# Keep x whole where it was first loaded, and take five of the eight row blocks of the residual sum from there instead of loading them a second time

## The reference, cut to what matters

```python
def L0(V, adj):      # N = 8192, D = 128
    return (adj == 1) @ (V @ w1) + (adj == 2) @ (V @ w2) + (adj == 3) @ (V @ w3) + bias
def L1(X, adj):
    h = X @ W.T + b
    e = leaky(h @ we1 + be1 + (h @ we2 + be2).T)      # slope 0.01
    return softmax(where(adj > 0, e, -9e15), axis=1) @ h
x = layernorm(x + L0(x, adj))
x = layernorm(x + L1(x, adj))
```

## Time and profile before

| what | value |
|---|---|
| median of 3 runs | 1555.93 us (1555.51 to 1557.21) |
| the profiled execution's own time | 1557.76 us |
| its span | 1556.1 us |
| PE busy | 1418.2 us, 91% |
| DVE busy | 1106.7 us, 71% |
| ACT busy | 981.2 us, 63% |
| mean granted TensorE clock | 0.979 |
| loads of 512 KB `x_rows<-x` | 8, median 7.2 us from issue to landing |

### The profile page before, as it was taken

How to read it: one execution, slowest core, us unless ns; L and a number is a source line. 1 busy time by engine, 2 the same in 40 slices (tenths; PEclk the granted TensorE clock), 3 DMA queues, 4 the chain that set the end, 5 groups by cost and what they waited for, 6 DMA issues and landing times. The chain is left out here.

```text
span 1556.1 us, 19556 instructions
## 1 busy us (share of the span) xinstructions
PE 1418.2 (91%) x6934; PEld 669.7 (43%) x6934; DVE 1106.7 (71%) x2561; ACT 981.2 (63%) x1584; POOL 102.2 (7%) x137
## 2 busy tenths in 40 slices
PE   0887798979999999999999997999999999999996
PEld 0434343444444444444444443444444444444443
DVE  2667777877977967967967946577667676666663
ACT  1334527446457457457457558678888788788873
POOL 2111111100110110100101000000000000000000
PEclk9989899999999999999999998999999999999998
DMA  9999999994979779886889421000110000100100
GB/s 125 145 126 116 130 107 140 115 108 76 83 100 115 83 74 102 114 83 75 113 85 102 82 95 55 8 1 28 48 34 28 28 28 27 55 27 28 35 1 15
DMA packets 88980, 114.32 MB, mean 73 GB/s; under 512 B 5104, under 2 KB 71216, under 8 KB 88880
## 3 DMA queue, kind: packets, MB, share of 16 engines
q0 software_dynamic: 67584, 67.12, 47.1%
q1 hardware_dynamic: 21296, 45.92, 8.6%
HBM read 298.06 MB, written 16.29 MB: 202 GB/s over the span
## 5 line engine op out<-in xcount | busy, mean ns | idle before, releaser
L1234 PE MATMUL ps<-pos_masks,tables 128*128 128x512 fp8e4 x2048 | 613.6, 381 | 39.6 <-DVE pos_masks L616 39.6
L1023 ACT ACTIVATE neg_masks<-e_row,cols 128x512 int8<-128x512 f32 x816 | 509.8, 709 | 109.0 <-PE ps L1234 58.4
L1234 PE MATMUL ps<-neg_masks,tables 128*128 128x512 fp8e4 x1632 | 489.7, 382 | 0.0
L1187 PE MATMUL ps<-edge_masks,tables 128*128 128x512 fp8e4 (+1 forms) x2048 | 463.9, 385 | 0.0
L1234 PEld LDWEIGHTS ps<-pos_masks,tables 128*128 128x128 f16 x2048 | 199.6, 98 | 285.8 <-issue 57.0
L1187 PEld LDWEIGHTS ps<-edge_masks,tables 128*128 128x128 f16 x2048 | 201.6, 99 | 233.2 <-issue 13.3
L1234 PEld LDWEIGHTS ps<-neg_masks,tables 128*128 128x128 f16 x1632 | 160.6, 98 | 195.8 <-issue 5.5
L614 DVE TENSOR_TENSOR neg_masks<-pos_masks,neg_masks 128x2048 uint16<-128x2048 uint16 x102 | 125.0, 1225 | 92.6 <-ACT neg_masks L1023 89.9
L598 DVE TENSOR_SCALAR pos_masks<-edges 128x512 uint16<-128x512 uint16 x512 | 114.4, 286 | 89.4 <-PE ps L1234 89.4
L1002 ACT ACTIVATE packed_bf<-packed 128x1024 bf16<-128x1024 uint8 x64 | 72.3, 1130 | 149.4 <-DVE packed L588 149.4
L598 DVE TENSOR_SCALAR edge_masks<-edges 128x512 uint16<-128x512 uint16 x512 | 124.2, 308 | 54.4 <-PE ps L1187 53.4
(11 more groups left out here) (134 smaller groups left out, 850.5 us busy)
## 6 DMA issues: line engine op xcount, KB each, us to landing
adj_in<-adj POOLq DMA_DIRECT2D x84, 512.0 KB, 13.7
tables<-adj POOLq DMA_DIRECT2D x28, 512.0 KB, 32.3
e_row<-e_scratch SPq DMA_DIRECT2D x34, 256.0 KB, 3.9
edges<-adj POOLq DMA_DIRECT2D x16, 512.0 KB, 12.5
part_scratch<-a_c_rows SPq DMA_DIRECT2D x18, 256.0 KB, 4.1
part_in<-part_scratch SPq DMA_DIRECT2D x18, 256.0 KB, 3.1
edges<-x SPq DMA_DIRECT2D x8, 512.0 KB, 6.6
x_rows<-x SPq DMA_DIRECT2D x8, 512.0 KB, 7.2
```

Source lines behind the costliest of these rows:

```text
L1023: ins = e.activation(gate_bufs[GATE[m]][:, n:n + GR].bitcast(I8), e1row[:, q % 2, :], ACT.Sign, bias=t2[:, JC * c + j:JC * c + j + 1])
L1187: ins = e.matmul(ps[:, h, :], v_hl[:, i, JC * c + j, :], U0[:, n:n + GR].bitcast(kind), start=c == 0 and j == 0 and i == 0, stop=c == NCH ...
L1234: ins = e.matmul(z_bank(q, k), tab[:, c, 2 * k + i, j, :], mask[:, n:n + GR].bitcast(F8A), start=first and j == 0 and i == 0, stop=final a ...
```

## The change

`split_rest` no longer writes over `x_in`. It writes the rest into `yT8`, which is the buffer `yT` (`y_turned` in the trace, free until slot 9) seen as 8 x 128, and `split_low` reads it there. There is one such buffer for all eight pieces, so `split_rest(v)` also waits until `split_low(v - 1)` is done. `x_in` stays whole until `edges_of` writes edge blocks 4 to 7 over it. `x_and_bias(S)` for S below `KEPT = 5` reads `x_in`, and the five loads `xg_load(0)` to `xg_load(4)` are gone; those for S = 5, 6 and 7 stay. `edges_of(k)` from k = 32 on waits for four, from k = 48 on for five `x_and_bias`. As `xg` is now written by DVE where a transfer wrote it, `x_and_bias(S)` waits for `e_sums(S - 1)`.

```diff
--- before.py
+++ after.py
@@ -105,6 +105,8 @@
 ASK = [max(-1 if p is None else p for p in LAST[:k + 1]) for k in range(K)]
 GUEST = {n: max(k for k in range(K) if HOME[k] == n) for n in (2, 3, 4)}
 AFTER = 9
+
+KEPT = 5
 
 STAGED = (4, 5, 6)
 
@@ -383,7 +385,6 @@
                 if v > 1:
                     e.wait_ge(s_adj[HOME[v - 2]], 32 * FILL[v - 2])
                 x_piece(v)
-            xg_load(0)
 
             def tail(S):
                 e.wait_ge(s_x1, S + 1)
@@ -399,7 +400,8 @@
                         e.dma_start(tab_dram[S - 4, n], (yT, xg)[n][:, :, :].rearrange("p a b -> p (a b)"))\
                             .then_inc(s_tabst, 16)
                     e.wait_ge(s_tabst, 16 * (2 * (S - 3)))
-                xg_load(S + 1)
+                if S + 1 >= KEPT:
+                    xg_load(S + 1)
 
             def row_of(q):
                 g = SEGS[q][0]
@@ -566,7 +568,8 @@
             def split_rest(v):
                 sl = slice(v * JC, (v + 1) * JC)
                 e.wait_ge(s_vh, v + 1)
-                e.tensor_tensor(x_in[:, sl, :], x_in[:, sl, :], v_hl[:, 0, sl, :], ALU.subtract).then_inc(s_vr, 1)
+                ge(e, s_vl, v)
+                e.tensor_tensor(yT8, x_in[:, sl, :], v_hl[:, 0, sl, :], ALU.subtract).then_inc(s_vr, 1)
 
             def check_and_pack(k):
                 e.wait_ge(s_adj[HOME[k]], 32 * FILL[k])
@@ -617,9 +620,15 @@
 
 
             def x_and_bias(S):
-                e.wait_ge(s_xg, 16 * (S + 1))
+                if S < KEPT:
+                    e.wait_ge(s_x, 16 * (S + 1))
+                    ge(e, s_er, S)
+                    rows = x_in[:, S * JC:(S + 1) * JC, :]
+                else:
+                    e.wait_ge(s_xg, 16 * (S - KEPT + 1))
+                    rows = xg[:, :, :]
                 e.wait_ge(s_w, W_ALL)
-                e.tensor_tensor(xg[:, :, :], xg[:, :, :], biases[:, 0:D].unsqueeze(1).broadcast_to([P, RB, D]),
+                e.tensor_tensor(xg[:, :, :], rows, biases[:, 0:D].unsqueeze(1).broadcast_to([P, RB, D]),
                                 ALU.add).then_inc(s_xb, 1)
 
             def v_of(S, h):
@@ -994,7 +1003,7 @@
             def split_low(v):
                 sl = slice(v * JC, (v + 1) * JC)
                 e.wait_ge(s_vr, v + 1)
-                e.activation(v_hl[:, 1, sl, :], x_in[:, sl, :], ACT.Copy, scale=LOW).then_inc(s_vl, 1)
+                e.activation(v_hl[:, 1, sl, :], yT8, ACT.Copy, scale=LOW).then_inc(s_vl, 1)
 
             def convert(k):
                 e.wait_ge(s_pk, k + 1)
@@ -1006,6 +1015,7 @@
                 e.wait_ge(s_turn, k + 1)
                 if k >= 4 * NCH:
                     e.wait_ge(s_vl, NCH)
+                    e.wait_ge(s_xb, KEPT if k >= 6 * NCH else 4)
                 if k >= (NS - 1) * NCH:
                     e.wait_ge(s_pk, GUEST[4] + 1)
                 e.activation(bits_of(k // NCH, k % NCH), psT, ACT.Copy).then_inc(s_evac, 1)
```

## The result

| | before | after |
|---|---|---|
| median of 20 runs each, us | 1555.95 | 1553.67 |
| lowest and highest, us | 1552.58, 1558.86 | 1550.6, 1556.67 |
| span of the profiled execution, us | 1556.1 | 1554.1 |
| mean granted clock of PE | 0.979 | 0.979 |

The ratio of after to before is 0.9985, with a 95% interval from 0.9978 to 0.9992. The changed kernel is 2.3 us faster (1.2 to 3.4), where 2.0 had been forecast. The interval does not reach no change; the forecast had held anything under 0.2% (3.1 us) for too small to tell.

A forecast was written before the change was run, and what follows sets the result against it. Up to 142 us the DMA engines set the slot time, behind that the chain through DVE, ACT and PE. -1.3 - 0.7 = -2.0 us takes 1555.93 to 1553.9 us; range 1552.0 to 1556.4 us.

The forecast's parts named there:

- The removed load of block 0: At chunk 6, where DVE waits for each chunk: it comes 1.32 us sooner and the shift stays, -1.3 us.
- The first rival: In slot 6 the chunk loads need something besides DMA engines, so freed time stays empty: 1555.2 to 1555.9 us, chance 0.14.
- A sooner landing of the first `e_row`: Around 159 us, without `xg_load(1)` behind it, the load ACT waits for lands sooner: -0.7 us.
- I take half of the upper end: At the first `e_row`: upper end 1.5 us (4.5 against 3.0 us) for 512 KB behind; 256 KB follows now, so 0.7 us.
- The other four loads: Loads of blocks 1 to 4, where DVE never waits for a chunk: worth 0, but for the first of them.
- it is hidden by the work of slots that take longer than 9.90 us: Up to 778 us: the 5.3 us of transfer of blocks 1 to 4 counts as 0.
- Added waits, other buffer: In `split_rest`, `x_and_bias` and `edges_of`: new waits already met, subtraction still 1223 ns, cost 0; at worst 1.3 us for asking.
- The slower rival: `edges_of(32)` hangs on `x_and_bias(3)`, deciding if DVE comes over 6.5 us later against ACT: 1557.4 us if 10 late, chance 0.04.
- the larger gain: At slot 13, ACT's 2.98 us wait gone and PE perhaps keeping its clock: 4.3 or 7.2 us, some 1551.6 us, chance 0.17.
- The rival of unlucky meetings: Saved time returns as another wait, e.g. `e_row` meeting a chunk load, up to 2.9 us: around 1555.9 us, chance 0.07.
- The growth behind 190 us: Sign against the forecast: a kernel difference growing after 190 us, forecast as -2.0 us there and at the end.

The follow-up runs named there:

- kept1: Against the kernel before, only the load of block 0 is removed, with the added waits of `edges_of` left: 1555.48 us, ratio 0.9993.
- load0_back: The changed kernel with the load of block 0 put back, its data unused: 1554.73 us, ratio 0.9985 to the kernel before.
- load0_again: The changed kernel with the load of block 0 put back, timed a second time: 1553.72 us, ratio 0.998 to the kernel before.
- after_again: The changed kernel, unaltered, measured once more: 1552.62 us, ratio 0.9976 to the kernel before on the same chip.
- kept0_timed: The kernel before with all eight loads, only the subtraction's target and the waits of `split_low` and `edges_of` changed: 1556.92 us, ratio 1.0.

## Why the prediction was right in its sum and wrong in two terms

- **The removed load of block 0, -1.3 us: right.** Every trace without this load has a slot 5 of 11.23 or 11.24 us, and every one with it 12.56 to 12.58. Four loads more cost four times the price. The first rival, that the DMA engines lose what they win, fell here. Alone the load is worth 1.1 us by the ratio of `kept1` (from 2.5 us gained to 0.3 lost), which agrees but would not have shown it.
- **A sooner landing of the first `e_row`, -0.7 us: wrong.** The step that failed is "I take half of the upper end", above all the upper end itself, read from a pair taken on emptier DMA engines: their share was 0.74 in the 4.5 us from 368.5 us and 0.25 in the 3.0 us from 723.1 us, against 1.11 in the 6.0 us from 159 us. On full ones the load takes 5.9 to 6.3 us with anything or nothing behind it. The rule of the Trainium skill, DMA: Bandwidth & Descriptors, section Queues, rings and completion order, which I had weighed lower, agrees with the runs there. On emptier engines the landing did get shorter without the load of `x` behind (4.5 us at 368.5 us before, 3.3 us after; 4.0 to 4.9 us in six traces with the load behind and 3.0 to 3.3 us in five without), nearly as the upper end had it, but no engine waited for it.
- **The other four loads, 0: wrong.** The step that failed is "it is hidden by the work of slots that take longer than 9.90 us". The medians of kernels without them, against those with them, give: `load0_back` -2.5, `load0_again` -3.2, `after_again` against `kept1` -2.9, and the first measurement -2.3 + 1.3 = -1.0 us. So they are worth some 1 to 3 us, less than the 5.3 us that they would cost on a stretch that waits for the DMA engines. That DVE waits for a chunk only once behind 142 us only shows that chunks are early; ACT stands idle there for `e_row` loads, 14.43 us at 326 us and 7.78 us at 431 us in the trace of before.
- **Where those 1 to 3 us are is open.** They rest on the timed runs alone. The four loads were issued between 159 and 492 us, and from the start of chunk 6 to that of chunk 63 the six traces with them take a mean of 789.8 us (1.80 us taken off for `four_more`) and the five without 789.6: the traces do not show the gain where the loads stood. The profiled executions are single ones and need not be typical: that of `load0_again` took 1555.34 us, its median is 1553.72; that of `kept0_timed` 1555.13 us, its median 1556.92. The spans of six traces with the four loads, each set to the same state of load 0 by 1.33 or 5.33 us, have a mean of 1554.6 us; those of five without have 1553.6. But single spans in each group differ by up to 4 us, 1.7 us of scatter is there before chunk 5 starts, and slot 13 (21.95 to 23.6 us), slot 19 (11.0 or 12.5) and slot 25 (21.8 to 24.1) each scatter as much as the whole effect.
- **One way that would fit, and what speaks against it.** The `e_row` loads for which ACT waits might land sooner without the four loads, but where that can be seen it gave nothing: the one issued at some 425 us, for which ACT stands idle 5.9 to 8.7 us, landed after a mean of 6.6 us with the four loads and 5.5 without, and yet slots 31 and 32 together took 32.2 and 32.1 us. At 318 us the landings were 5.6 to 7.4 us with and 5.1 to 7.0 us without.
- **Added waits, other buffer: 0, right.** `kept0_timed` is at 1.0, the subtraction takes 1225 instead of 1223 ns, and the gap with four semaphores is 0.04 us. The slower rival had its condition, DVE 6.5 us late against ACT, never met: the lead was 7.25 us. Nor was that of the larger gain: ACT's wait for the first `e_row` was 2.98 us before and 3.28 after, not gone. The rival of unlucky meetings took the `e_row` loads in full stretches to land after 5.9 us and others after 3.0 to 4.5; they scatter more than that, up to 9.9 us at 159.86 us, and such scatter is what slot 25 shows, in both kernels.
- **The growth behind 190 us.** The forecast named it as a sign that the hidden loads were not hidden. It came (-0.66 to -2.77 us in slot 25), but it showed nothing: repeats of both kernels had it the other way round. That the hidden loads are worth something came from the timed runs.

The two wrong terms, -0.7 too much and some 1 to 3 us too little, nearly cancelled in the first measurement. That its sum came within 0.3 us of the forecast was luck in this part; in the second, at -4.4 us, they did not cancel.

## What to carry to other kernels

Where an engine waits for transfers in every slot, the difference between the cadence with and without a load is its price, and it held for one load and for five. Where nobody waits for that transfer, a removed one may still be worth a part of its time, though no run here shows by what way; look at what stands behind it in the same queue before writing 0. A price for a wait should be read from rows taken under the same load of the DMA engines. A long idle stretch whose wait has no releaser deserves a look at the order of the queue that feeds it: moving a load ahead of a store it did not depend on gave 13 us, where removing five loads gave 2.3 and 4.4 us in two measurements.

## What the runs showed of the hardware

- A 512 KB load beside the stream of chunks costs 1.33 us of it, one at a time or five at once, in the stretch where DVE waits for every chunk.
- A 256 KB load on full DMA engines took 5.9 to 6.3 us at one place, whatever stood behind it, and 5.1 to 7.4 us at another, up to 1.9 us apart in two executions of one program. On nearly idle ones it took 3.0 us.
- With a 512 KB load ahead of it in the same queue it took 9.9 us, with a 256 KB load ahead 7.8, with nothing ahead 6.2.
- The granted clock behind a short pause of PE came out as 1.00 in one execution and as 0.82 in another of one program, and the slot was 1.5 us longer.
